# Layer 1's exponentials: half transposed by TensorE and summed in fp32, half split in rows and transposed by DMA

## The reference, cut to what matters

```
h = x @ W
e = leaky_relu((h @ a_src)[:, None] + (h @ a_dst)[None, :])       # layer 0
att = softmax(where(valid, e, NEG)); att = where(att >= 1e-4, att, 0) * L
x = layernorm(x + elu(h + att @ h))

s = leaky_relu(x @ ks.T)                                          # layer 1
attn = softmax(where(adj > 0, s, -9e15))
x = layernorm(x + attn @ ks)
```

## Time and profile before

| what | value |
|---|---|
| median of three runs | 855.38 us |
| the profiled execution, its span | 855.3 us |
| TensorE busy | 827.0 us (97%) |
| VectorE busy | 788.1 us (92%) |
| ScalarE busy | 760.6 us (89%) |
| GpSimd busy | 224.9 us (26%) |
| DMA queue of GpSimd, share of 16 engines | 53.5% |
| DMA queue of SP, share of 16 engines | 12.7% |

### The profile page before, as it was taken

The page is one execution under the profiler, slowest core; times in us unless marked ns, Lnnn a source line. Parts: engine busy times, 40 slices in busy tenths (PEclk is TensorE's granted clock), DMA queues, the critical chain, the costliest instruction groups (busy, mean ns, idle before and its releaser), DMA issues.

```text
span 855.3 us, 17732 instructions
## 1 busy us (share of the span) xinstructions
PE 827.0 (97%) x7139; PEld 714.2 (84%) x7139; DVE 788.1 (92%) x1009; ACT 760.6 (89%) x732; POOL 224.9 (26%) x446
## 2 busy tenths in 40 slices
PE   7489999999999999999999999999999999999997
PEld 7468888888998888889888888988888898888876
DVE  3999999999999999999999999999999999997865
ACT  2899999999999999999999999999999999998763
POOL 2033232323312233332223333222233321222100
PEclk9799999999999999999999999999999999999999
DMA  9999786666688766668866667886666678611000
GB/s 212 239 131 172 151 149 102 122 130 131 141 155 148 106 120 130 132 139 154 151 104 122 130 131 139 153 153 104 126 124 136 135 151 155 103 31 24 13 2 10
DMA packets 39969, 106.07 MB, mean 124 GB/s; under 512 B 11088, under 2 KB 23504, under 8 KB 32208
## 3 DMA queue, kind: packets, MB, share of 16 engines
q0 software_dynamic: 20864, 66.06, 53.5%
q1 hardware_dynamic: 18592, 38.80, 12.7%
q10 hardware_dynamic: 432, 0.07, 0.1%
HBM read 138.48 MB, written 2.10 MB: 164 GB/s over the span
## 4 chain that ended last, share of the span: by engine, by line
PE 83%; DVE 9%; ACT 4%; issue 2%; DMA 1%; POOLq 0%; POOL 0%; ACTq 0%; DVEq 0%
PE work L290 23%; PE sums L410 23%; PE sums L438 12%; PE work L381 6%; PE work L382 6%; PE work L386 6%; PE sums L439 6%; DVE att1T L996 2%; DVE att L908 2%; ACT att L677 1%; ACT att L634 1%; PE sums L444 1%; PE work L315 1%; ACT att L654 1%; ACT att0T L666 1%
## 5 line engine op out<-in xcount | busy, mean ns | idle before, releaser
L290 PE MATMUL work<-ident,att 128*128 128x128 f32 x2072 | 256.2, 275 | 14.0 <-DVE att L1098 12.6
L290 PEld LDWEIGHTS work<-ident,att 128*128 128x128 f32 x2072 | 233.6, 142 | 22.7 <-DVE att L1098 13.0
L410 PE MATMUL sums<-h_all,att0T 128*128 128x128 f32 x2048 | 244.2, 275 | 0.0
L410 PEld LDWEIGHTS sums<-h_all,att0T 128*128 128x128 f32 x2048 | 236.1, 192 | 0.1
L438 PE MATMUL sums<-k_parts,att1T 128*128 128x257 f16 x1024 | 182.3, 274 | 0.3 <-DVE att1T L996 0.2
L439 PE MATMUL sums<-k_parts,att1T 128*128 128x129 f16 x1024 | 177.3, 218 | 0.0
L996 DVE SCALAR_TENSOR_TENSOR att1T<-work,att1T 128x1024 f16<-128x1024 f32 x128 | 152.3, 1209 | 12.9 <-ACT att1T L687 12.8
L687 ACT ACTIVATE att1T<-work 128x1024 f16<-128x1024 f32 x127 | 129.4, 1029 | 27.9 <-PE work L290 27.9
L921 DVE SCALAR_TENSOR_TENSOR att<-att,cut 128x2048 f32<-128x2048 f32 x62 | 145.2, 2346 | 0.0
L672 ACT ACTIVATE att<-work 128x1024 f32<-128x1024 f32 x128 | 127.7, 1028 | 19.5 <-PE work L386 19.5
L960 DVE CUSTOM_DVE_ANT_0 att<-att,mask 128x2048 f32<-128x2048 f32 x62 | 141.3, 2282 | 2.0 <-ACT att L672 2.0
(11 more groups left out here) (123 smaller groups left out, 669.6 us busy)
## 6 DMA issues: line engine op xcount, KB each, us to landing
mask<-adj POOLq DMA_DIRECT2D x31, 1024.0 KB, 8.6
mask_zero<-zero_cols SPq DMA_DIRECT2D x29, 1024.0 KB, 5.0
mask_zero<-adj POOLq DMA_DIRECT2D x29, 1024.0 KB, 11.7
att<-x SPq DMA_DIRECT2D x4, 512.0 KB, 6.7
k_parts<-ks POOLq DMA_DIRECT2D x2, 1024.0 KB, 19.7
x_sb<-x SPq DMA_DIRECT2D x32, 64.0 KB, 2.8
out<-x SPq DMA_DIRECT2D x32, 64.0 KB, 4.8
mask<-adj POOLq DMA_DIRECT2D x2, 512.0 KB, 6.6
```

The costliest lines, as they stand in the source:

```text
L290: mm = pe.transpose(place[:, b * P:(b + 1) * P], source(c * PER + b), ident[:, :])
L410: mm = pe.matmul(acc0, att0T[:, k * P:(k + 1) * P], h_all[:, k, :], start=(k == 0), stop=(k == BLOCKS - 1))
```

## The change

- With `WHOLE = 2`, chunks 0 and 1 of layer 1 are still transposed by TensorE, but `copy1` writes them as fp32 and `sum1` multiplies them in fp32 with a new fp32 tile `k_whole` (ks and a column of ones, 129 columns).
- For chunks 2 and 3 ScalarE writes the fp16 high part before any transposing, in one instruction of 2048 columns (`split_high`, into `high1`), VectorE writes the low parts over `att1` itself, as fp16, both into the place of chunk 3 (`low_part1`, `low_at`), and SP transposes them by DMA (`turn_high`, then `turn_low` of chunk 3 and of chunk 2).
- `sum1` of a split block has three fp16 products of 129, 128 and 129 columns. There is one accumulator of 129 columns, and `finish1` has one instruction fewer.
- `turn_high(u)` waits until `sum1(u-1, 3)` is done, since its target has one buffer. `bend1(t, 3)` waits until both `turn_low` of the tile before have landed, since they read `att1`.
- New orders: all of `sum1` is done one slot later (tile t-2 in slot t). On ScalarE `split_high` stands between `copy1(u, 1)` and `elu_exp(t)`. On VectorE `build_mask` stands ahead of `normalise0`, and `finish1` behind both `low_part1`. The first score waits for all four low parts of ks.
- `early_slots` and `last_slots` are gone: every tile from 1 on takes the plain slot, and a short `last_layer` ends it. The last tile is transposed by TensorE throughout.

```diff
@@ SP
+            def turn_high(u):
+                sp.wait_ge(high_ready, u + 1)
+                if u > 0:
+                    sp.wait_ge(summed1, 4 * u)
+                else:
+                    sp.wait_ge(k_turned, CHUNKS)
+                sp.dma_start_transpose(high1T.rearrange("p (b r) -> p b r", r=P), high1[:, :]).then_inc(high_turned, 16)
+
+            def turn_low(u, c):
+                sp.wait_ge(low1, SPLIT * u + LOW_ORDER.index(c) + 1)
+                sp.dma_start_transpose(low1T[:, split_part(c)].rearrange("p (b r) -> p b r", r=P),
+                                       att1_halves[:, low_at(c)]).then_inc(low_turned[c], 16)
...
+                if 1 <= t < TILES:
+                    turn_high(t - 1)
+                    for c in LOW_ORDER:
+                        turn_low(t - 1, c)
@@ TensorE, sum1
+                if c < WHOLE:
+                    pe.wait_ge(copied1, WHOLE * u + c + 1)
+                    for k in range(c * PER, (c + 1) * PER):
+                        mm = pe.matmul(acc, whole1T[:, k * P:(k + 1) * P], k_whole[:, k, :], start=(k == 0), stop=False)
+                else:
+                    if u < TILES - 1:
+                        pe.wait_ge(high_turned, 16 * (u + 1))
+                        pe.wait_ge(low_turned[c], 16 * (u + 1))
+                    else:
+                        pe.wait_ge(low1, SPLIT * u + c - WHOLE + 1)
+                    for k in range(c * PER - WHOLE_BLOCKS, (c + 1) * PER - WHOLE_BLOCKS):
+                        part = slice(k * P, (k + 1) * P)
+                        pe.matmul(acc, high1T[:, part], k_parts[:, k, 0:D + 1], start=False, stop=False)
+                        pe.matmul(acc[:, 0:D], high1T[:, part], k_parts[:, k, D + 2:], start=False, stop=False)
+                        mm = pe.matmul(acc, low1T[:, part], k_parts[:, k, 0:D + 1], start=False, stop=(k == SPLIT_BLOCKS - 1))
@@ TensorE, slot
                 turn0(t, 2)
+                if w >= 0:
+                    sum1(w, 0)
                 sum0(t, 0)
                 turn0(t, 3)
                 sum0(t, 1)
                 sum0(t, 2)
-                turn1(u, 0, True)
+                turn1(u, 0)
                 sum0(t, 3)
-                turn1(u, 1, True)
+                turn1(u, 1)
+                if w >= 0:
+                    sum1(w, 1)
                 if w >= 0:
                     sum1(w, 2)
+                turn_q(t)
+                if w >= 0:
                     sum1(w, 3)
-                turn1(u, 2, True)
-                turn1(u, 3, True)
-                sum1(u, 0)
-                turn_q(t)
-                sum1(u, 1)
-                for c in range(3):
-                    score(t, c)
+                score(t, 0)
+                score(t, 1)
+                score(t, 2)
@@ ScalarE
+                if u > 0 and c < WHOLE:
+                    act.wait_ge(turned1, WHOLE * (u - 1) + c + 1)
+                elif u > 0:
+                    act.wait_ge(low1, SPLIT * (u - 1) + LOW_ORDER.index(c) + 1)
+                    for low in LOW_ORDER:
+                        if low_at(low).start // (2 * CHUNK) == c:
+                            act.wait_ge(low_turned[low], 16 * u)
...
+            def split_high(u):
+                act.wait_ge(exp1, 2 * u + 2)
+                if u > 0:
+                    act.wait_ge(high_turned, 16 * u)
+                nc.scalar.activation(high1[:, :], att1[:, WHOLE_COLS:N], ACT.Copy, scale=LIFT).then_inc(high_ready, 1)
...
                 copy1(u, 0)
                 copy1(u, 1)
+                split_high(u)
                 elu_exp(t)
                 if t + 2 < TILES:
                     bend0(t + 2)
-                copy1(u, 2)
                 q_high_part(t)
-                copy1(u, 3)
@@ VectorE
+                nc.vector.scalar_tensor_tensor(att1_halves[:, low_at(c)], att1[:, cols(c)], LIFT, high1[:, split_part(c)],
+                                               ALU.mult, ALU.subtract).then_inc(low1, 1)
...
                 residual0(t)
-                low_part1(u, 0)
                 elu(t)
+                if EARLY <= t + 1 < TILES:
+                    build_mask(t + 1)
+                normalise0(t)
+                low_part1(u, 3)
+                q_low_part(t)
+                low_part1(u, 2)
                 if w >= 0:
                     finish1(w)
```

More of the change, by code:

```diff
@@ L124, in graph_layers @@
         rstd0 = pair("rstd0", [P, 1])
-        x1 = pair("x1", [P, D])
+        x1 = [sb(f"x1_{i}", [P, D]) for i in range(3)]
+        wT_sb = x1[2]
         qT = sb("qT", [P, 2, P], F16)
-        res1_half = pair("res1_half", [P, D])
         res1 = pair("res1", [P, D])
@@ L220, in graph_layers, with place, low_at, split_part @@
         H_FILLS = -(-BLOCKS // H_PER)
-        K_PLACE = (2, 0, 1, 2)
+        FILLS = ([("turn0", 0, c) for c in range(CHUNKS)] + [("k", 0, c) for c in range(CHUNKS)]
+                 + [("score", 0, c) for c in range(3)])
+        for tile in range(1, TILES):
+            FILLS += ([("score", tile - 1, 3)] + [("turn0", tile, c) for c in range(CHUNKS)]
+                      + [("turn1", tile - 1, c) for c in range(WHOLE)] + [("score", tile, c) for c in range(3)])
+        FILLS += [("score", TILES - 1, 3)] + [("turn1", TILES - 1, c) for c in range(CHUNKS)]
+        FILL_INDEX = {fill: n for n, fill in enumerate(FILLS)}
+        def place(kind, tile, c):
+            return work[:, (FILL_INDEX[kind, tile, c] + 1) % SLOTS, :]
+        def low_at(c):
+            last = CHUNKS - 1
+            lo = 2 * last * CHUNK + (last - c) * CHUNK if c >= last - 1 else (2 * last - 1) * CHUNK
+            return slice(lo, lo + CHUNK)
+        def split_part(c):
+            return slice((c - WHOLE) * CHUNK, (c - WHOLE + 1) * CHUNK)
         def place_of(kind, i):
@@ L287, in _, with turn, wait_place @@
         def _(pe):
[L288 removed]
+            def turn(into, c, source):
                 for b in range(PER):
[L290 removed]
+                    mm = pe.transpose(into[:, b * P:(b + 1) * P], source(c * PER + b), ident[:, :])
                 return mm
+            def wait_place(kind, tile, c):
+                n = FILL_INDEX[kind, tile, c]
+                if n < SLOTS:
+                    wait_emptied(*(("d", 3), ("d", 2), ("z", 3))[n])
+                    return
+                before, of, part = FILLS[n - SLOTS]
+                if before == "turn0":
+                    pe.wait_ge(copied0, 4 * of + part + 1)
+                elif before == "k":
+                    pe.wait_ge(kT_low, part + 1)
+                elif before == "score":
+                    pe.wait_ge(bent1, 4 * of + part + 1)
+                elif part < WHOLE:
+                    pe.wait_ge(copied1, WHOLE * of + part + 1)
+                else:
+                    pe.wait_ge(low1, SPLIT * of + part - WHOLE + 1)
             def wait_emptied(kind, i):
@@ L434, in sum1 @@
                         pe.wait_ge(k_low, 16)
-                        pe.wait_ge(k_one_ready, 1)
-                for k in range(c * PER, (c + 1) * PER):
-                    part = slice(k * P, (k + 1) * P)
-                    pe.matmul(acc, high1T[:, part], k_parts[:, k, 0:2 * D + 1], start=(k == 0), stop=False)
-                    mm = pe.matmul(acc[:, D:], low1T[:, part], k_parts[:, k, D:2 * D + 1], start=False, stop=(k == BLOCKS - 1))
+                        pe.wait_ge(k_one_ready, 2)
@@ L599, in last_slots, with last_layer @@
+                score(t, 0)
+                score(t, 1)
+                score(t, 2)
+            def last_layer():
+                last = TILES - 1
+                score(last, 3)
+                for c in range(CHUNKS):
+                    sum1(last - 1, c)
+                turn1(last, 0)
+                turn1(last, 1)
+                turn1(last, 2)
                 sum1(last, 0)
-                turn1(last, 3, False)
+                turn1(last, 3)
                 sum1(last, 1)
@@ L708, in k_high_part @@
                 act.wait_ge(k_turned, c + 1)
-                nc.scalar.copy(kT[:, 0, cols(c)], work[:, K_PLACE[c], :]).then_inc(kT_high, 1)
+                nc.scalar.copy(kT[:, 0, cols(c)], place("k", 0, c)).then_inc(kT_high, 1)
             def to_first_slot():
```

504 lines of the change are left out of this document (105 added, 399 removed).

## The result

The changed kernel takes **1093.76 us** (median of 4 runs, 1091.23 to 1098.28) against 856.17 (4 runs of the kernel before): a ratio of 1.279, 95% interval 1.275 to 1.282. Slower, as forecast, but by 238 us instead of 90, and above the range. The profiled run has a span of 1094.0.

What follows compares the result with a forecast made beforehand. TensorE bounded the kernel before; after the change the small chain stalls it 2.8 us a slot. First score 60.4 + tile 1's slot 25.2 + 30 x 27.8 + tail 26.5 = 946, stated as 945 us; range 880 to 1085.

Steps and rivals of the forecast that it cites:

- the tail: From the last tile's first score to the end of the kernel: 26.5 us, as before within 1 us.
- S: Start of turn1(u,1) on TensorE, behind the tile's last sum0; turn_q was predicted at S + 6.84 us.
- elu_exp to turn_q: VectorE's aggregate and build_mask, 2.55 us, then the hop from normalise0 to turn_q, 0.39 us.
- clock: TensorE's stall before turn_q lowers its clock for the scores, costing 1.7 us; taken in half the slots, 0.8 us.
- score to next S: TensorE's work in the rest of the slot, 18.5 us, with no wait if the transposes land in time.
- TensorE's work: Per slot 24.87 - 1.75 (two transposed chunks gone) + 0.91 (fp32 products) = 24.03 us.
- copy1 at 324.90 = S + 1.07: On ScalarE in the small chain: copy1's start 1.07 us after S, read from the kernel before.
- GpSimd's deviation ends at 328.30, 2.48 after elu_exp, so it hides behind the mask: In the small chain: GpSimd's deviation adds nothing, as VectorE's aggregate and build_mask take 2.55 us after elu_exp.
- rival 3: Chain holds the slot, clock stays up: 27.0 us, 922; clock down everywhere 28.7, 973. Counted within the forecast's 0.50.
- rival 1: Transposes gate bend1(t,3): each microsecond landing beyond 5.9 costs 30 us; 1008 at 8, 1083 at 10.5. Chance 0.34.
- at that time the other queues are mostly idle, because GpSimd's loads come later: At the transposes after the score: reason for taking the lower row, 1 MB landing in 5.0 us without stall.
- rival 2: TensorE stays the bound, the small chain does not hold it: slots of 24.03 us, 833 us. Chance 0.08.

Runs made afterwards that it cites:

- e11: e10 with GpSimd's accumulating load of adjacency moved ahead of coefficient(t+1) in its list: 924.6 us.
- e8: The changed kernel with low transposes issued ahead of the high one, and sum1(w,1) moved right behind sum1(w,0): 1040.1 us.
- e2: The changed kernel with build_mask(t+1) moved from ahead of normalise0 to behind the second low_part1 on VectorE: 1108.3 us.
- e4: The changed kernel with 38 fp16 products, whose result nobody reads, added on TensorE just before turn_q: 1098.1 us.
- after: The changed kernel itself, with no further edit, against the kernel before: 1093.76 us.
- e10: The changed kernel with e2's and e8's edits, low transposes first, and ScalarE's and VectorE's queues reordered to TensorE's needs: 1042.9 us.
- e12: e11 with GpSimd's plain load of adjacency also moved ahead of coefficient(t+1), behind the accumulating one: 920.0 us.
- e9: e4 with GpSimd's two adjacency loads cut to a sixteenth of their columns from tile 4 on, output not the reference's: 1037.6 us.

## Why the prediction was wrong

The sum ended at 946; 1094 is 148 more. By its terms, the first score comes at 57.4 instead of 60.4 (-3.0: it waits for the fourth low part of ks, as said, but that is no later than the score was before), the slot of tile 1 28.7 instead of 25.2 (+3.5), the tail is 27.2 instead of 26.5 (+0.7), and 30 slots take 32.69 each instead of 27.8 (+146.6). So it is the slot, 4.89 us of it. The rows but the last are the common slot of 31.86 us shown above:

| term, us a slot | predicted | measured | difference |
|---|---|---|---|
| S to turn_q: copy1(u,1) late | 1.07 | 2.92 | +1.85 |
| elu_exp behind it | 2.83 | 2.72 | -0.11 |
| elu_exp to turn_q | 2.94 | 3.78 | +0.84 |
| turn_q to score, at full clock | 1.66 | 1.62 | -0.04 |
| clock (sum1(w,3) +1.23, scores +0.61) | 0.8 | 1.84 | +1.04 |
| score to next S, but for the clock | 18.5 | 18.98 | +0.48 |
| longer slots, spread over all | 0 | 0.83 | +0.83 |

**TensorE's work: right.** Split products stand 0.055 to 0.06 apart, a chunk of 129 fp32 columns takes 506.32 - 504.53 = 1.79 as worked out from the earlier trace rows, and the rest after the score is within 0.5 us. e11's short slot, 25.63 with a stall of 1.43, leaves 24.2, which is 0.17 above the 24.03 of the sum.

**The failed step in the chain: "copy1 at 324.90 = S + 1.07".** I carried over a row of the kernel before, where another wait ended last. After the change copy1(u,1) writes into whole1T, which sum1(w,1) still reads, and the new slot order puts sum1(w,1) behind turn1(u,1). Both facts stood in the diff: one buffer, and the order of two lines. Measured, copy1(u,1) starts at S + 2.92; e8 shows the 1.85 us of chain. No run shows what the slot would be with a second buffer and the product left in its place, so how much of the slot it is rests on the sum alone. I had priced the same reads for TensorE and not for the buffer.

**The second failed step: "GpSimd's deviation ends at 328.30, 2.48 after elu_exp, so it hides behind the mask".** It doesn't hide; it is slowed by it. In the kernel before it was over (328.30) when the mask began (330.36); here its first instruction takes 1.10 us beside build_mask and 0.22 without (e2). The Trainium skill (SBUF — State Buffer, section Who interferes with whom) states the rule: while VectorE runs in a mode that uses both of its port pairs, GpSimd is shut out for the whole instruction, and the other way round. The traces agree: the instruction of 1.10 us ends at 511.98, just behind the mask's end at 511.90. By that page, and by the durations of the earlier trace rows, the sum would have been some 0.8 us a slot higher, which is an estimate.

**The clock: right mechanism, wrong size.** I took it in half of the slots and on the scores. It falls in every slot, and most of it is paid in sum1(w,3) (2.58 us instead of 1.35), which stands right behind the stall. The granted clock is 0.50 there, 0.77 from S to the score, and 1.00 in the steady slot of the earlier trace rows. e4 shows 1.5 us of the 1.84 by filling the hole. "The clock down in every slot" stood as rival 3's upper edge, 973.

**The transposes: rival 1, in part.** The failed step is "at that time the other queues are mostly idle, because GpSimd's loads come later". That is so of this slot's loads. Those of the slot before are the ones that meet the transposes: GpSimd issues them 9 to 19 us behind the score (13 to 14 in common slots), and they need 13 and 18 us to land (their medians in after). They come so late because small instructions ahead of them in its list take 2.4 to 4.6 us beside VectorE's large ones, 0.2 to 1.3 in the kernel before; that is argued from durations, as no run removes it. One of them, with the two instructions of VectorE beside it:

```profile
517.36 3.32 POOL L1166 TENSOR_SCALAR var<-mv 128x1 f32<-128x1 f32 x1 [4.72 <-DVE mv L891]
```
```profile
517.19 2.32 DVE L793 SCALAR_TENSOR_TENSOR att<-att,cut 128x2048 f32<-128x2048 f32 x1
519.43 1.22 DVE L771 TENSOR_SCALAR mask_zero<-mask_zero 128x4096 bf16<-128x4096 bf16 x1
```

In a common slot the loads end just in time (0.5 us lost); in five of 30 they don't, and the sixth long slot is open. In after this term is only 1.3 of the 4.89 us, but e2, e4 and e10 show its nature: each saving elsewhere shortens the time between the loads and the next transposes, and more slots become long ones. Rival 1 would have cost 1008 by a landing at 8; the low ones landed near 6.7 in common slots and at 8.0 to 11.0 in the six long ones. The direction of its mechanism held; that the *issue* on SyncE's queue is stretched, and not only the transfer, I had not thought of.

**Why the range failed.** 1085 was rival 1 with a landing at 10.5 and all else as forecast. Three terms were off in the same direction, and they are not independent: the longer chain makes the hole, the hole makes the clock fall. I had priced the rivals one at a time.

**Would the change pay with everything repaired?** Not by the runs, and by the sum not by much: a slot without collisions is 25.63 (e11, e12's last ones), 0.76 above the 24.87 of the earlier trace rows, because 1.43 us of stall are left against 0.84 us of saved work. What a stall of zero would give (rival 2, 833) wasn't reached by any run.

## What to carry to other kernels

Where a change alters the order, don't carry a start time over from the old trace: for each instruction of the chain list all its waits, the one for the buffer it writes among them, and ask which comes last in the new order. A transfer added at a fixed point of the slot is priced against what was issued well before it (here up to 14 us), in the slot before too, not against what its neighbours in the program issue. And when a saving of one microsecond makes the slot longer by five, look for two transfers that have moved onto each other: moving one `dma_start` gave 118 us here (some 101 without one odd slot), more than e10's reordering of all queues, which gave 51.

## What the runs showed of the hardware

- The issue of a transposing DMA of 0.5 MB occupied SyncE's queue for 1.65 us in a common slot, and for 3.6 to 6.8 us in after and e4 with two 1 MB loads of GpSimd issued 11 to 14 us before it; that of the two low ones took 9.64 us with loads 6 us before them. With the loads cut to 64 KB each issue was 1.2 to 2.1 us (e9, from tile 13 on). A plain DMA is not stretched in this way: the issue of the 1 MB of zeros on the same queue stays at 0.46 to 0.55 us in after, though beside the loads it lands after 11.0 us (median) and not after 5.0.
- The Trainium skill (Advanced Engine Details and Errata, section X-Bar Transpose (TRN2)) calls transposing DMAs as fast as regular ones. Without large loads the traces come near it: in e9 the three together, 1 MB, have landed 6.3 us after the first issue, against 5.0 for the plain 1 MB.
- A 128x1 instruction of GpSimd took 0.22 us alone (e2) and 1.10 beside one of VectorE on bf16 in SBUF. Another took 3.32 where VectorE had an instruction with two fp32 inputs and then one on bf16; it ended at 520.68, the second of these at 520.65.
- 38 useless products before turn_q lifted the mean granted clock from 0.90 to 0.96 and took 1.5 us from each undisturbed slot.
